# Attention with cosines on one core: two chunks' scores in one block, four masked buffers, and a turn moved behind the second key product

## What is computed in stage 5

```
Qp = relu(x @ Wq + bq);  Kp = relu(x @ Wk + bk);  V = x @ Wv + bv
Qc, Qs = Qp * cosw, Qp * sinw;   Kc, Ks = Kp * cosw, Kp * sinw
def step(carry, inp):            # over the tokens
    S_cos = S_cos + kc[:, None] * v[None, :]     # and S_sin likewise
    z_cos = z_cos + kc                           # and z_sin likewise
    num = qc @ S_cos + qs @ S_sin
    den = maximum(sum(qc * z_cos + qs * z_sin), 1e-6)
    return num / den
y = out.reshape(B, T, 16 * 64) @ Wo + bo
```

## Time and profile before

| | |
|---|---|
| median of 3 runs | 2793.97 us (2779.53 to 2797.71) |
| profiled execution, its own time | 2796.76 us |
| its span in the trace | 2795.0 us |
| stage 5 in that span | 705 to 1376 us, and its last output to about 1406 us |
| mean granted clock of TensorE over the span | 0.927 |

### The profile page before, as it was taken

The page is one execution under the profiler, slowest core; times in us unless marked ns, Lnnn a source line. Parts: engine busy times, 40 slices in busy tenths (PEclk is TensorE's granted clock), DMA queues, the critical chain, the costliest instruction groups (busy, mean ns, idle before and its releaser), DMA issues. The chain is left out here.

```text
span 2795.0 us, 35026 instructions
## 1 busy us (share of the span) xinstructions
PE 2458.3 (88%) x12122; PEld 1771.0 (63%) x12122; DVE 1871.1 (67%) x3501; ACT 1478.0 (53%) x3113; POOL 968.7 (35%) x769
## 2 busy tenths in 40 slices
PE   6678677699899999999989999688888886999998
PEld 2555556587788888888866777333333333677776
DVE  6746555777566666666567565388888886866765
ACT  4321222498444444444355555565555553888787
POOL 1000000020222222222114555588888884222221
PEclk8668899899899999999979999899999998999999
DMA  4000000000000000000010000122222230000001
GB/s 174 0 1 0 1 1 1 1 1 1 16 1 1 1 1 1 1 1 1 1 61 1 1 1 8 50 80 80 80 81 80 82 89 19 1 1 1 1 1 31
DMA packets 31169, 66.85 MB, mean 24 GB/s; under 512 B 3200, under 2 KB 7312, under 8 KB 30480
## 3 DMA queue, kind: packets, MB, share of 16 engines
q1 hardware_dynamic: 30960, 64.59, 7.4%
q0 software_dynamic: 32, 0.02, 0.0%
HBM read 61.98 MB, written 2.62 MB: 23 GB/s over the span
## 5 line engine op out<-in xcount | busy, mean ns | idle before, releaser
L192 PE MATMUL ps<-TMPr 128*128 128x512 f32 (+6 forms) x3936 | 1030.9, 409 | 62.1 <-DVE TMPr L208 34.7
L192 PEld LDWEIGHTS ps<-TMPr 128*128 128x128 f32 (+4 forms) x3936 | 727.9, 191 | 376.2 <-issue 184.0
L212 POOL TENSOR_TENSOR TMP<-TMP 128x512 f32<-128x512 f32 (+2 forms) x480 | 612.4, 1300 | 683.0 <-ACT TMP L203 466.1
L192 PE MATMUL ps<-TMP 128*128 128x65 f32 (+5 forms) x4352 | 544.3, 292 | 1.2 <-DVE TMP L207 0.5
L192 PEld LDWEIGHTS ps<-TMP 128*128 128x128 f32 (+3 forms) x4352 | 486.8, 192 | 68.2 <-issue 26.7
L192 PE MATMUL ps<-TMP,W 128*128 128x512 f32 (+5 forms) x720 | 376.4, 646 | 103.0 <-POOL TMP L212 41.5
L203 ACT ACTIVATE TMP<-ps,W 128x256 f32<-128x256 f32 (+2 forms) x528 | 283.5, 584 | 339.2 <-DVE TMP L208 193.3
L208 DVE TENSOR_TENSOR TMP<-ps,TMP 128x512 f32<-128x512 f32 (+1 forms) x434 | 251.6, 604 | 143.2 <-ACT TMP L203 74.4
L192 PEld LDWEIGHTS ps<-TMP,W 128*128 128x128 f32 (+3 forms) x720 | 128.7, 197 | 273.6 <-issue 144.2
L203 ACT ACTIVATE TMPr<-ps,W 128x512 fp32r<-128x512 f32 x352 | 242.5, 689 | 110.2 <-PE ps L192 89.6
L212 POOL TENSOR_TENSOR XT<-XT,XK 128x512 f32<-128x512 f32 x128 | 175.5, 1371 | 319.0 <-DVE XK L211 305.8
(11 more groups left out here) (186 smaller groups left out, 2753.0 us busy)
## 6 DMA issues: line engine op xcount, KB each, us to landing
TMP<-rows SPq DMA_DIRECT2D x168, 256.0 KB, 3.6
W<-wp SPq DMA_DIRECT2D x1, 4124.0 KB, 13.5
W<-wp SPq DMA_DIRECT2D x1, 3072.0 KB, 25.2
W<-wp SPq DMA_DIRECT2D x1, 2136.5 KB, 18.4
XT<-xT SPq DMA_DIRECT2D x4, 512.0 KB, 5.5
out<-XK SPq DMA_DIRECT2D x8, 256.0 KB, 2.3
W<-wp SPq DMA_DIRECT2D x1, 1993.0 KB, 13.8
W<-wp SPq DMA_DIRECT2D x1, 903.0 KB, 9.5
```

Source lines behind the costliest of these rows:

```text
L192: return nc.tensor.matmul(out, lhsT, rhs, start=start, stop=stop, **k)
L212: gtt = lambda o, a, b, op: nc.gpsimd.tensor_tensor(o, a, b, op)
```

## The change

The scores of two chunks are issued together: at chunks 0 and 2 of each iteration the score step makes the scores of chunks s + 2 and s + 3 in one block of eight matmuls. The steps at chunks 1 and 3 are gone. Masked scores go into four buffers instead of two. The turn of the divided output moves from behind key product 0 to behind key product 1, and with the same line the output product moves from ahead of query product 2 to behind it.

```diff
-        AM = [ar(512) for _ in range(2)]
+        AM = [ar(512) for _ in range(4)]
...
                 for j in range(3 if c < 2 else 2):
                     take(nx)
-                    if j == 0 and c < 2:
+                    if j == 1 and c < 2:
                         take(nf)
...
-                if s + 1 < NS:
-                    plan.append(("score", s + 1))
+                if c % 2 == 0 and s + 2 < NS:
+                    plan.append(("score", s + 2))
                 plan.append(("out", s))
...
-        a_pe, a_dve = Sig(sem("s5_score_pe"), S), Sig(sem("s5_score_masked"), S)
+        a_pe, a_dve = Sig(sem("s5_score_pe"), of(plan, "score")), Sig(sem("s5_score_masked"), S)
...
-                    for h in range(4):
-                        r0 = 64 * (h % 2)
-                        r = mm(pscore[a % 2][:, h % 2, h // 2, :], hc(KT, h // 2, c)[r0:r0 + 64, :], hc(Qr, h, c)[r0:r0 + 64, :])
+                    for n in (a, a + 1):
+                        for h in range(4):
+                            r0, c = 64 * (h % 2), n % 4
+                            r = mm(pscore[n % 2][:, h % 2, h // 2, :], hc(KT, h // 2, c)[r0:r0 + 64, :], hc(Qr, h, c)[r0:r0 + 64, :])
                     r.then_inc(*a_pe(a))
...
-                    am, po = a4(AM[a % 2]), PS[5 + a % 2]
+                    am, po = a4(AM[a % 4]), PS[5 + a % 2]
...
                     e.wait_ge(*a_pe.at(a))
-                    if a >= 2:
-                        e.wait_ge(*o_pe.at(a - 2))
-                    tt(a4(AM[a % 2]), pscore[a % 2], dm, ALU.mult).then_inc(*a_dve(a))
+                    for n in (a, a + 1):
+                        if n >= 4:
+                            e.wait_ge(*o_pe.at(n - 4))
+                        tt(a4(AM[n % 4]), pscore[n % 2], dm, ALU.mult).then_inc(*a_dve(n))
```

More of the change, by code:

```diff
@@ L1549, in pe @@
                 elif step == "score":
-                    m, c = divmod(a, 4)
+                    m = a // 4
                     Qr, Qe, KT, Ke, Vv = sets[m % 2]
```

## The result

The changed kernel takes 2759.4 us (median of 4 runs, 2759.2 to 2762.7) against 2795.8 us (median of 4 runs, 2779.5 to 2799.7) for the kernel before. The ratio is 0.9875, with a 95% interval of 0.9857 to 0.9893: about 1.25% faster. Its profiled execution took 2759.3 us with a span of 2757.5, 37.5 less than before.

A forecast was written before the change was run, and what follows sets the result against it. TensorE's queue in stage 5 was taken as the bound. Half the score blocks (21.6 us) plus shorter waits (9.3 us) gave 31 us off the profiled 2796.8, a median forecast of 2763 us, with 8 in 10 within 2748 to 2782.

The forecast's parts named there:

- Part 1: TensorE's queue in stage 5: 64 score blocks instead of 128, each saving 0.34 us, 21.6 us in all.
- only entry and exit: Rival on score blocks: only entering and leaving 64-row mode is saved, 11.7 us, giving 2773 us; chance 0.17.
- Part 2: End of iteration: the mask leaves; TensorE's waits before were 25.4 us; weight splits, not the mask, are late next.
- the sum: Stage 5: 21.6 us from fewer blocks plus 9.3 us from shorter waits, 31 us saved.
- Part 3: Turn behind both key products: waits of 16.1 us remain of 25.4, so they shrink by 9.3 us.
- ScalarE's collision: Into an odd iteration the cast meets key 1's ACTIVATE, starting at 0.89 instead of 0.67; second turn waits 0.34 us.
- Value 1: On TensorE, waits for the bank queries 2 and 3 empty: about 0.1 us in 15 iterations, up to 0.4.
- three long waits: First turn at three odd-into-even places that also split the input: 1.84 us each before, 1.4 after.
- Waits back in full: Rival: cast, subtraction and queries come later, all 9.3 us of saved waits go, 2772 us; chance 0.12.
- no wait left: Rival: small shifts fall well, only the three long waits stay, 43 us saved, 2751 us; chance 0.10.
- The slower one: Rival: first turn's cast on ScalarE runs late, second turn 2 us later in 30 iterations, 2823 us; chance 0.03.

The follow-up runs named there:

- parted blocks: Changed kernel with each score block cut in two around the state, 64-row mode entered 127 times instead of 64: 2782.1 us.
- odd-chunk kernel: Changed kernel with its score blocks at chunks 1 and 3 instead of 0 and 2: 2759.5 us.
- kernel with later splits: Changed kernel with the splits of the next group's weights moved from the end of odd iterations to the end of even ones: 2752.7 us.
- both repeats: The kernel before, unchanged, profiled two more times: 2793.5 and 2796.7 us.
- scores alone: Changed kernel with the turn put back behind key product 0, leaving scores in pairs and four buffers: 2766.8 us, ratio 0.9905.
- turn alone: Kernel before with only the turn moved behind both key products, one score per chunk and two buffers kept: 2775.6 us, ratio 0.9933.
- last version: Changed kernel with weights split one iteration later and the second turn behind chunk 0's score block: 2745.0 us, ratio 0.9823 to the kernel before.

## Why the prediction was right

The forecast was 2763 us, in a range of 2748 to 2782; the measured median is 2759.4.

- **What bounds the kernel.** TensorE's queue in stage 5, as said. The part of the span outside the stage didn't move but for about 3 us.
- **Part 1**, 21.6 us for half as many blocks: right in mechanism and size. The steps in the block are those of the earlier trace rows, once a block, and 63 more blocks cost 23.3 us. With every step of the loop counted at its steady rate, the changed queue is 21.6 us shorter by my sum. The rival "only entry and exit" is out, by the steps within the block and by the parted blocks.
- **Part 2**, where the first turn's waits come from: right. The splits of weights, not the mask, are late behind an odd iteration; both the odd-chunk kernel (masks put back, nothing lost at the turn) and the kernel with later splits (waits gone) show it. One count was off: ahead of the last iteration no weights are left to split, so there are 14 such places in the loop and not 15 (20.9 us of waits before, where the sum had 21.2).
- **Part 3**: the first turn's waits were to be 7.8 us and are 7.7. The second turn's were to be 6.8 and are 3.3, the largest mis-sized term among the waits: 0.18 into an odd iteration where 0.34 was forecast, and 0.04 into an even one where it was 0.11. I gave ScalarE's collision 0.22 us and it took 0.12 (cast at 0.78 behind the turn, not 0.89), and I gave TensorE 0.15 us to take up the low part where it took 0.06 (905.08 + 0.69 = 905.77 to 905.83). Value 1 was to wait 1.5 us more and waits 1.1. The output product doesn't wait; before it waited 4.7 us and not 4.2. In all the waits by starts shrink by 28.6 - 15.1 = 13.5 us, against 9.3.
- **What the sum lacked** is the clock above all: 5.6 us in the last iteration, and some 1.7 us more in the loop: in the first profile of before and in both repeats (at 1184 to 1187 us) the clock stood at half for 3.4 us at one of the three long waits of the first turn; the changed kernel has no such stretch. About 2.3 us are given back behind the stage. Without the clock the loop is 35.0 - 1.7 = 33.3 us shorter, where the sum said 31. It also lacked the second matmul behind each late one, which comes 0.05 us late as well: there are more such places now, and they cost 1.6 us. So 21.6 + 13.5 - 1.6 + 1.7 gives the loop's 35.0 to within 0.2.
- **Where it was luck.** The mechanism holds, but the time is this near in part by chance. The change saves 36.5 us by the medians where 31 was forecast; the forecast started from a median of 2794.0 and the kernel before had 2795.8 in the end, so the time is only 3.6 us off. And misses cancel in part: 4.2 us of waits and 7.3 us of clock came on top, 1.6 us of late second matmuls and 3.1 us ahead of and behind the stage went off.
- **The rivals.** "Waits back in full" and "no wait left" are both out: 15.1 us of 28.6 are left. The slower one never came near its point, a second turn that waits 1 us; it waits 0.1.

## What to carry to other kernels

Where an engine is full, count what each switch of its mode costs between the starts of its instructions, not in busy time: here a block of four short matmuls cost 0.79 us and the four more behind it only 0.45. When a step is moved away from a wait, follow the chain that hangs on it: the second turn took back 3.3 us, and moving that one too brought another 5.6. And ask what else stands in the late engine's queue; the mask looked guilty, the weight splits were.

## What the runs showed of the hardware

- Going from 128-row to 64-row matmuls costs more than the entry: 0.21 to the first pair, 0.21 to the second, 0.21 back and 0.16 to the next, against 0.112 steady, 0.34 us in all. Entry and exit alone would be 0.18, and the parted blocks show that at least the whole 0.34 is paid. The Trainium skill (TensorEngine Tiling (Array Packing), Key Properties) says that a change of the tiling mode drains TensorE; the slow entry and exit agree with that.
- The granted clock fell from 2.4 to 1.2 GHz for 10 us in the last iteration of the kernel before, in three profiles of three, and not there in the changed one, though the 1.0 us wait at the first turn of that iteration is in both. What the engine did before differs: the loop of before stood still for 0.4 to 0.8 us in every iteration. No run here settles why, and the kernel with the scores alone stands still as often and kept its clock there. Shown is only that the fall repeats with the kernel in profiles. The mean clock of its other executions lies between 0.924 and 0.935, and the ones at 0.933 and above took 2785 to 2790 us, so it may be that not every execution has the same falls.
- The low clock at the start of the stage does not always end at the same place: it ended 10.0 to 10.1 us after the first key product in the kernels with the scores alone, the turn alone, the parted blocks, the odd chunks and the later weights, and 13.1 to 13.3 us after it in both main kernels and in the last version. The 3.2 us at half clock are worth some 1.6 us. In the profiles where it ended early, that was ahead of the stage's first score block (11.2 us after the first key product in the parted blocks), which is the first step on TensorE that any edit touches. So no edit explains the difference; its cause is open.
